# Moving vector-engine work between the slots of an adaLN, two-direction Mamba and mixture-of-experts block

## What is computed

```python
mod = silu(c) @ wmod                      # six rows per batch: sa, ca, ga, sb, cb, gb
h = layernorm(x) * (1 + ca) + sa
xn = layernorm(h) * norm_g + norm_b
def mamba(x):                             # 256 inner channels, 16 states
    u, z = split(x @ Win.T)
    u = silu(causal_conv4(u) + convb)
    dtr, B, C = split(u @ Wx.T)
    dt = softplus(dtr @ Wdt.T + bdt)
    for t: s = exp(dt[t] * A) * s + dt[t] * u[t] * B[t];  y[t] = s . C[t]
    return ((y + u * D) * silu(z)) @ Wout.T
x = x + ga * (h + mamba_f(xn) + flip(mamba_b(flip(xn))))
h2 = layernorm(x) * (1 + cb) + sb
w = softmax over the top 2 of (h2 @ gate_w), 0 elsewhere      # 8 experts
x = x + gb * (sum_e w[e] * swiglu_e(h2) + swiglu_shared(h2))
```

## Time and profile before

| | us |
|---|---|
| median of 3 runs | 2323.21 (2323.15 to 2324.65) |
| profiled execution, its own time | 2322.59 |
| its span, first to last instruction | 2320.8 |
| DVE busy | 2184.6 (94%) |
| POOL busy | 2018.6 (87%) |
| PE busy | 1994.2 (86%) |
| ACT busy | 1511.7 (65%) |

### The profile page before, as it was taken

How to read it: one execution, slowest core, us unless ns; L and a number is a source line. 1 busy time by engine, 2 the same in 40 slices (tenths; PEclk the granted TensorE clock), 3 DMA queues, 4 the chain that set the end, 5 groups by cost and what they waited for, 6 DMA issues and landing times. The chain is left out here.

```text
span 2320.8 us, 28426 instructions
## 1 busy us (share of the span) xinstructions
PE 1994.2 (86%) x8357; PEld 1121.6 (48%) x8357; DVE 2184.6 (94%) x3338; ACT 1511.7 (65%) x2499; POOL 2018.6 (87%) x1334
## 2 busy tenths in 40 slices
PE   5678988989889898988979899897988989798778
PEld 2444454545545454454544545454554545445443
DVE  5999999999999999999999999999999999999962
ACT  4656666676666767666676666667666676766533
POOL 2778989989898998989899898998989899897955
PEclk8679999999999999999999999999999999999999
DMA  5434444444354444435344443444435344443411
GB/s 156 140 138 141 156 136 144 140 143 151 127 170 133 143 142 142 163 121 167 132 146 140 148 158 130 150 141 143 151 123 174 128 147 142 143 158 119 162 50 42
DMA packets 130703, 323.75 MB, mean 139 GB/s; under 512 B 22260, under 2 KB 46820, under 8 KB 130548
## 3 DMA queue, kind: packets, MB, share of 16 engines
q1 hardware_dynamic: 130548, 321.93, 42.1%
HBM read 315.28 MB, written 6.60 MB: 139 GB/s over the span
## 5 line engine op out<-in xcount | busy, mean ns | idle before, releaser
L517 POOL TENSOR_TENSOR bt<-v,bb 128x1024 f32<-128x1024 f32 x511 | 1208.4, 2368 | 83.3 <-DVE psA L976 69.3
L976 DVE TENSOR_TENSOR_SCAN psA<-psA,bt 128x512 f32<-128x512 f32 x1024 | 1195.7, 1213 | 33.8 <-ACT psA L710 33.1
L710 ACT ACTIVATE psA<-dt,aneg 128x512 f32<-128x512 f32 x1024 | 689.1, 688 | 672.8 <-DVE g L986 671.7
L1232 PEld LDWEIGHTS psY<-ident,g 128*128 128x128 f32 x4096 | 487.8, 146 | 476.3 <-DVE g L986 281.1
L1232 PE MATMUL psY<-ident,g 128*128 128x128 f32 x4096 | 580.8, 284 | 159.0 <-DVE g L986 157.6
L986 DVE TENSOR_TENSOR g<-psA,cb 128x512 f32<-128x512 f32 x1024 | 671.4, 675 | 0.0
L1366 PE MATMUL F<-h2T,w 128*128 128x512 f32 x576 | 327.2, 651 | 119.8 <-DVE pf L1076 117.1
L618 POOL TENSOR_TENSOR act<-pf,gf 128x512 f32<-128x512 f32 x288 | 370.3, 1286 | 53.8 <-DVE pf L1076 43.9
L1403 PE MATMUL F<-act,w 128*128 128x512 f32 x576 | 281.0, 593 | 0.4 <-POOL act L618 0.4
L1248 PE MATMUL psP<-xnT,wcT 128*128 128x512 f32 x496 | 242.9, 613 | 0.1
L1076 DVE SCALAR_TENSOR_TENSOR pf<-tf,F 128x512 f32<-128x512 f32 x288 | 194.5, 675 | 40.9 <-ACT tf L797 37.2
(11 more groups left out here) (185 smaller groups left out, 1846.7 us busy)
## 6 DMA issues: line engine op xcount, KB each, us to landing
bb<-bc_rows SPq DMA_DIRECT2D x256, 512.0 KB, 4.6
cb<-bc_rows SPq DMA_DIRECT2D x256, 512.0 KB, 3.7
wB<-w_rows SPq DMA_DIRECT2D x128, 256.0 KB, 4.8
x<-in_L_attn_x SPq DMA_DIRECT2D x16, 256.0 KB, 4.5
out_x<-osb SPq DMA_DIRECT2D x16, 256.0 KB, 4.4
modA<-mod_table SPq DMA_DIRECT2D x15, 192.0 KB, 4.7
w<-in_L_ffn_ew SPq DMA_DIRECT2D x2, 1024.0 KB, 7.6
bc_rows<-xd SPq DMA_DIRECT2D x32, 64.0 KB, 3.0
```

The costliest lines, as they stand in the source:

```text
L517: g.tensor_tensor(bt[:, n % 2, :, :], v[d][:, :, :], bb[:, n // 2 % 2, n % 2, :].unsqueeze(1).broadcast_to([P, NH, T]), ALU.mult).then_inc ...
L710: s.activation(psA[:, half * T:half * T + T], dt_[d][:, half, :], ACT.Exp, scale=aneg[d][:, half, n:n + 1]).then_inc(a_s, 1)
L976: w.tensor_tensor_scan(ah, ah, bt[:, n % 2, half, :][:, order], 0.0, ALU.mult, ALU.add)\
L1232: last = m.matmul(psY[:, half * T + i * P:half * T + i * P + P], g_[:, n % 2, half, i * P:i * P + P], ident[:, :], is_transpose=True, star ...
```

## The change

1. **Gate products of direction 0.** `gate_y(b, 0, half)` stood in slots 17 and 18 (one each), both halves turned by PE into `psP`. Now both stand in slot 29; half 0 is turned into `F1`, half 1 into `psP`. The projection of z for the next batch into `F1` (slot 30) now also waits for the first product (`gF_s`).
2. **Down products.** `DOWN_SLOTS` has two each in slots 17 and 18 (one each before) and one in slot 29 (three before).
3. **Statistics of x.** Four `bn_stats`, a memset and four `bn_aggr` stood in slot 29. Now two `bn_stats` each stand in slots 10 and 11, writing a tile of their own `stX`, and the four `bn_aggr` in slot 0 of the next pass. x is loaded in slot 3 instead of 20. The memset is left out in all statistics.
4. **Router.** DVE keeps `max`, `max_index`, and one comparison of 64 columns, in slot 8, where it had two of 32 in slot 7. The difference of the two top values goes to POOL (slot 8), the cast of the indices to ACT (slot 8), the copy of the second value is gone.
5. **hx.** It has two buffers; ACT's copy `hxK` (slot 6) is gone, and POOL's product for it stands in slot 29, ahead of `make_dt`, instead of slot 22.
6. **Last pass.** Odd expert halves use the two halves of `psA` in place of `F0`/`F1`; the second turn of direction 1 goes into `psA`; the part of the output projection that belongs to direction 0 is done in slot 30 of pass 15, into `psP`; the router's product stands behind the first up product; the output is one DVE addition straight from `F1`.
7. **Start.** The two z projections of batch 0 go to `F2` and `F0`, ahead of the x projection.

The core of the diff:

```diff
-STAT_SLOT, RSTD_SLOT, ... = 29, 2, 3, 4, 10, 11, 12, 14
-X_SLOT = 20
-HX_SLOTS, WG_SLOT = (22, 1), 6
+STAT_SLOTS, AGGR_SLOT = {10: (0, 1), 11: (2, 3)}, 0
+X_SLOT = 3
+HX_SLOTS, WG_SLOT = (29, 1), 6
-POST_F_SLOT = 17
+POST_F_SLOT = 29
+LAST_PROJ_SLOT = 30
-DOWN_SLOTS = [10, 11, 15, 16, 17, 18, 20, 21, 24, 28, 28, 28, 29, 29, 29, 30, 30, 31]
+DOWN_SLOTS = [10, 11, 15, 16, 17, 17, 18, 18, 20, 21, 24, 28, 28, 28, 29, 30, 30, 31]
...
+        def up_banks(fb, k):
+            if fb == NB - 1 and k % 2:
+                return psA[:, 0:T], psA[:, T:2 * T]
+            return F0[:, :], F1[:, :]
...
 # POOL, slot 8
+                    pool.wait_ge(gate_s, GATES * fb + NT)
+                    g.tensor_tensor(gd[:, :], top[:, :, 1], top[:, :, 0], ALU.subtract).then_inc(gd_s, 1)
 # ACT, slot 8
-                        act_e.wait_ge(gate_s, GATES * (b - 1) + GATE_D)
+                        act_e.wait_ge(gd_s, b)
                         s.activation(ge[:, :], gd[:, :], ACT.Exp).then_inc(ge_s, 1)
+                        act_e.wait_ge(gate_s, GATES * b)
+                        s.activation(topf, topi[:, :, 0:2], ACT.Copy).then_inc(hot_s, 1)
...
 # PE, slot 29
+                    pe.wait_ge(z_free, 4 * b + 4)
+                    wait(pe, F1_free, UPS * b)
+                    turn(F1, 0, 0, False).then_inc(yF_s, 1)
+                    pe.wait_ge(pP_free, post_piece(b))
+                    turn(psP, 0, 1, False).then_inc(pP_full, 1)
...
 # PE, up products
-                    wait(pe, pf_s, at)
+                    used = at - 1 if fb == NB - 1 and k else at
+                    wait(pe, pf_s, used)
...
 # DVE, at the very end
+            dve.wait_ge(fin_s, NB)
+            dve.wait_ge(out_d, 16 * (NB - 1))
+            w.tensor_tensor(osb[:, :, :], F1[:, :]..., x2[:, :, :], ALU.add).then_inc(o_s, 1)
```

More of the change, by code:

```diff
@@ L148, in adaln_mamba_moe @@
         xnT = sb("xnT", [D, T + 2 * PAD])
-        hx = sb("hx", [P, NT, D])
-        hxK = sb("hxK", [P, NT, D])
+        hx = [sb(f"hx{k}", [P, NT, D]) for k in range(2)]
         wg = sb("wg", [P, 2, NH, D])
@@ L288, in adaln_mamba_moe @@
         gate_s = sem("gate_s")
+        gd_s = sem("gd_s")
         ge_s = sem("ge_s")
@@ L747, in prep @@
                     q = 5 * (2 * b + d)
-                    take(b, piece(d, DT, half))
+                    take(piece(b, d, DT, half))
                     wait(act_e, dt_s, 2 * b + d)
@@ L901, in body @@
                         ln1p(b, 1)
-                    if scan:
-                        if slot == X2_SLOT + 2:
-                            wait(act_e, F2_free, FREES * (b - 1) + PROJ + 1)
-                            act_e.wait_ge(hx_s, 2 * b + 2)
-                            s.activation(hxK[:, :, :], hx[:, :, :], ACT.Copy).then_inc(hxK_s, 1)
                     if slot == COPY_SLOT and b >= 2:
@@ L993, in statistics, with pieces_statistics, whole_statistics @@
                 dve.wait_ge(sig, q + NT)
-                w.memset(stat_[:, :, 4], 0.0)
                 for i in range(NT):
                     w.bn_aggr(stat_[:, i, 0:2], st_[:, i, :]).then_inc(sig, 1)
+            def pieces_statistics(b, slot):
+                dve.wait_ge(x_in, 16 * b + 16)
+                for i in STAT_SLOTS[slot]:
+                    w.bn_stats(stX[:, i, :], x[b % 2][:, i, :]).then_inc(lnA, 1)
+            def whole_statistics(b):
+                dve.wait_ge(lnA, 16 * b + NT)
+                wait(dve, zA, 8 * b)
+                for i in range(NT):
+                    w.bn_aggr(stat[:, i, 0:2], stX[:, i, :]).then_inc(lnA, 1)
             def first_statistics(b):
@@ L1392, in ffn_late @@
                         last.then_inc(F2_full, 1)
-                if slot == GATE_SLOT:
-                    pe.wait_ge(F2_free, free + GATE)
-                    for i in range(NT):
-                        last = m.matmul(F2[:, i * NX:(i + 1) * NX], h2T[:, i * P:i * P + P], gate_w[:, :],
-                                        start=True, stop=True)
-                    last.then_inc(F2_full, 1)
+                if slot == GATE_SLOT and fb < NB - 1:
+                    router(fb)
                 for k in downs_at(slot):
@@ L1447, in body @@
                         side(b, slot, True, None if last else b + 1, True)
+                    if b == NB - 1 and slot == LAST_PROJ_SLOT:
+                        pe.wait_ge(gF_s, NB)
+                        pe.wait_ge(pP_free, PIECES * NB)
+                        pe.wait_ge(wg_s, NB)
+                        last_projection(range(NH))
                     if ffn:
                         expert_up(b - 1, slot)
+                        if not scan_ and slot == GATE_SLOT:
+                            router(b - 1)
             passes(pe, body)
```

186 lines of the change are left out of this document (107 added, 79 removed).

## The result

The changed kernel takes 2287.03 us (median of 4 runs, 2286.41 to 2287.43), beside it the kernel before 2323.71 (2323.15 to 2324.65): a ratio of 0.9842, 95% interval 0.9824 to 0.9859. The forecast was 2291, range 2284 to 2303. The profiled execution took 2286.41 us, its span 2284.6. Such a reading rests on one profiled execution of each kernel.

What follows compares the result with a forecast made beforehand. DVE, busy 2147.26 of the scans' 2190.48 us, was taken as the bound. 2322.6 - 21.6 (scans) - 10.5 (last pass) = 2290.5; with the median 0.6 above the profiled execution, 2291 us, range 2284 to 2303.

Steps and rivals of the forecast that it cites:

- Slots 17 and 18: Scans, passes 1 to 14: each slot loses a gate product at 0.61 us, -1.21 us per pass.
- Slot 29: Gains two products (1.21 us), loses statistics (1.27); ACT's two table loads end it either way, PE in time: 0.
- Slots 10, 11, 0: Statistics moved in: slot 10 hides them, slot 11 pays 0.1, slot 0 0 to 0.1; sum +0.1 us per pass.
- Router: Slot 7 loses copy and other router work, -0.60 us; slot 8 gains one 64-column comparison, +0.15, per pass.
- `hx`, `hxK`, load, memset: POOL's `hx` fits in slot 29, x loads earlier, ACT's copy goes where ACT is not late: 0; memsets left out.
- Give back: Scans: 0.1 us per pass returned for small new waits of PE and of the router, +1.5 us in all.
- Pass 15: Slots 17, 18 and router -1.21 - 0.45; slot 29, without statistics or tables, grows from 3.76 to about 4.63: -0.8 us.
- Last pass: Second gate product -1.1, projection -1.9, inside experts -6.3 (middle term), end -1.2: sum -10.5 us (-12 to -6).
- PE late in slots 17 to 21: Rival: PE backlogs make ACT, then DVE wait; returns 0.7 us per pass, 2301; chance 0.10.
- "Only moved": Rival: rooms in slots 29, 10, 11, 0 are not room; -1.56 per pass becomes about -0.65, 2304; chance 0.06.
- this rival: Router turns late: `ge` waits for POOL, `tf` 0.6 us later; 0.3 to 0.6 us per pass, 2295 to 2300; chance 0.06.
- the fourth rival: PE's lower clock reaches slots full of PE work, one 4.3 us slot becomes 8.6, 2360; chance 0.03.

Runs made afterwards that it cites:

- The experiment: Changed kernel with direction 0's gate products back in slots 17 and 18, one down product there and three in slot 29: 2304.25 us, ratio 0.992.
- the experiment: Changed kernel with one down product each in slots 17 and 18 and three in slot 29, gate products staying in slot 29: 2293.99 us, ratio 0.9878.
- the copy ahead of `h2T`: Changed kernel with one `hx` buffer, ACT's copy `hxK` in slot 6, POOL's `hx` product in slot 22 and the memset back: 2292.13 us, ratio 0.9868.
- the same kernel with the copy behind: Changed kernel with the `hx`, `hxK` and memset edits undone, but copy `hxK` issued behind copy `h2T`: 2286.12 us, ratio 0.984.
- the two kernels whose edit touches only the last pass: Changed kernel with last-pass expert halves using F0 and F1 again: 2295.98 us; changed kernel with the last pass's router product first: 2285.08 us.
- the shorter ACT chain: Changed kernel with the softplus exponential between the scan exponentials' halves: 2281.66 us; that plus the router on DVE: 2288.06 us.
- the better version: Changed kernel with softplus exponential between scan exponentials (passes with experts), last-pass router first, slot 11's `bn_stats` in slot 29: 2278.60 us, ratio 0.9806.

## Why the prediction was right, step by step

- **Slots 17 and 18**, -1.21 per pass: -1.20. The step between starts, 0.61, was the right price. The experiment gave 17.2 us where I expected 18. By the sentence of the Trainium skill that the prediction names (VectorE: DVE Perf Modes, "The DRAIN you can't avoid") it would have been -1.38; the rows of the changed kernel, with starts 0.59 to 0.60 apart (1199.20, 1199.79, 1200.38), disagree with it again. The same section goes on to say that a next operation that is not held starts earlier, which I had passed over and which agrees with these rows.
- **Slot 29**, 0: right, and so was the reason that ACT's tables end it. That PE would turn in time I had taken from its count of down products; the experiment showed that this hung on them by 0.64 us, against my own forecast for that run.
- **Slots 10, 11, 0**, +0.1: slot 10 nothing, slot 11 +0.08, slot 0 nothing.
- **Router**, -0.45 per pass: -0.60 and +0.12, then -0.13 in slot 9 by its median (-0.09 in the mean), which I had not seen. I looked only for whether `tf` would be late in slot 8; I did not ask what the comparison of slot 8 gives ACT as a head start in slot 9.
- **`hx`, `hxK`, load, memset**, 0: right for all but the copy. The step "ACT's copy goes where ACT is not late" asked about ACT alone and not who stands behind the copy: `h2T` does, and PE waits for it. Beside the shorter slot 7 the copy ahead of `h2T` costs 5.1 us against the changed kernel and 6.0 against the same kernel with the copy behind. So a term put at nothing carried the router's gain: without this part of the change slot 9 would have taken most of it back.
- **Give back**, +1.5 for small waits: mis-sized by its source. The waits that came are those in slots 9 and 13 under the lower clock, 0.3 to 0.4 us in about eight passes, but slot 9 had such waits before the change too (4.45 for 4.15 in six passes), so little was lost anew. Passes 1 to 14 gave -24.4 where the forecast, with this term, had -20.3. Of the 4.1 between them this term is 1.5, slot 9 1.2 and the statistics in slots 10, 11 and 0 1.1, since they cost 0.35 in all and not 1.4; slots 8, 12 and 13 and other small differences are the rest. Pass 0 gave -0.67 (forecast -0.5, it lost 0.14 in slot 7 too) and pass 15 -0.14 (forecast -0.8): in all -25.2 against -21.6. So the sum came near by terms that erred both ways.
- **Pass 15**, -0.8: the profiled run shows -0.14. The terms themselves came as forecast (slots 17 and 18 -1.20, slots 7 and 8 -0.47, slot 29 +0.88), but slot 9 gave -0.43 and slots 11, 13 and 23 took +0.35, +0.51 and +0.20. In the two kernels whose edit touches only the last pass, pass 15 was 0.9 us shorter than before, without the delays of slots 13 and 23. The term stands; the delay in slot 11 I did not follow.
- **Last pass**, -10.5: -10.6. From the last scan's end to `x2` -2.85 (forecast -3.0), from the router or first up product to the last down product 60.18 to 53.82, -6.36 (forecast -6.3), the end -1.36 (forecast -1.2). The middle term was right for half its reason. The nine waits went in full, -7.3, and a smaller one with them; 1.4 came back ahead of the router's weights, whose wait grew from 0.23 to 1.60 us. That the start hangs on the weights the prediction said; that POOL would set the pace, its other reason for taking -6.3 and not -7.3, did not happen: no up product waits from 2236.72 on. That the two came out at -6.4 together is in part luck.

Rivals: PE late in slots 17 to 21 did not come; those slots take 4.02 to 4.03. "Only moved" fell with slot 29. The router turns a little later by way of POOL, as this rival says: in slot 8 of pass 8 ACT waits 0.53 us for POOL's difference. It costs nothing there, since DVE is busy through all 4.23 us of the slot. But something like this rival lives in slot 9: its mechanism is PE's lower clock, which the fourth rival had in slots full of PE's work. It costs 0.37 us where it lands, and not a slot of 8.6 for one of 4.3.

## What to carry to other kernels

Time that one engine waits is room for work only if what ends the wait doesn't depend on that work: take the work out (slot 29 kept its 5.29 us) or double it, and look whether the slot's length moves. A slot that gets shorter takes slack from every engine that works in it, and this slack may be what absorbs a disturbance elsewhere, so look at the next slots and at single passes, not at medians alone. When an instruction is costed at nothing because its engine is idle, ask also what stands behind it on that engine, and who waits for that.

## What was not expected of the hardware

The lower level of PE's clock comes at a place that drifts from pass to pass. In the changed kernel's profiled run the granted clock of slot 8 was 0.62 to 0.70 in passes 3 to 5 and 11 to 13, that of slot 13 was 0.58 to 0.67 in passes 1, 2, 7, 8, 9 and 15, and both were 1.00 in passes 6, 10 and 14. PE's idle time just before doesn't tell the passes apart: ahead of the router's product it is 0.78 us in pass 11, with the lower level behind it, and in pass 14, without. Whether it costs anything depends on the slack: 0.37 us in slot 9 in one kernel, 0.8 to 0.9 with one copy of 0.52 us more ahead of PE's input, nothing with 0.6 us more time in slot 7 and no such copy, and 0.06 to 0.09 with the shorter ACT chain, 0.06 to 0.22 in the better version that has it too. Why the place drifts was not tested. The memsets that left cost nothing measurable, slots 4 and 10 being as long with them (5.35 and 5.29).
